# The seam between an expert stage and an attention: queries and scores earlier, transposes later, last down products in two parts

## The chip, the cores and the metric

The kernel runs on one core of one Trainium2 chip. The core has TensorE (PE in the rows; PEld is its weight load), VectorE (DVE), ScalarE (ACT), GpSimd (POOL) and SyncE (SP), which issues most transfers. The engines run side by side and wait for one another by semaphores. The metric is the time of one launch in microseconds on the device; three runs of the kernel before gave 2293.72, 2294.40 and 2299.11 us, median 2294.4.

## The reference

The program is four residual layers on x, four batches of 512 tokens with 512 channels, in float32. The change lies between the second and the third.

```python
x = x + xattn0(layernorm(x), ctx)                      # layer 1: channel attention
xf = layernorm(x)                                      # layer 2: mixture of experts
top_p, top_i = top_k(softmax(xf @ gate_w.T), 2)        #   8 experts, 2 per token, inner width 352
y = sum_e combine[:, e] * (silu(xf @ fc1[e].T) * (xf @ fc2[e].T)) @ proj[e].T
x = x + y + sigmoid(xf @ shared_gate_w.T) * shared(xf)
q = layernorm(x) @ Wq                                  # layer 3: cross-attention, 16 heads of 128
k, v = ctx @ Wk, ctx @ Wv                              #   8 key heads, each for 2 query heads
x = x + softmax(mask(q @ k.T / sqrt(128))) @ v @ Wo
x = x + ffn(layernorm(x))                              # layer 4
```

## The kernel before, in words

**Precision.** Every product is made of three matmuls (`product`, L81 to L86): each operand is split into a high and a low part, high = a rounded copy, low = operand minus high. So each operand costs one copy (mostly ScalarE) and one subtraction (VectorE or GpSimd), and TensorE waits for the second.

**The expert stage** (`sparse_experts`) walks over 24 tiles of sorted tokens: two of 256 slots (two sub-tiles), then one of 128, and so on; tile 23, the last, is small. In step t TensorE does gate and up products of tile t, turns the gathered rows of tile t + 1, and does the down products of tile t - 1, sub-tile by sub-tile. A small tile's hidden values come out the other way round and are transposed (`turn_hidden`, L1686) before ScalarE's `hidden_high` and VectorE's `hidden_low` split them. Each down result is copied by ScalarE (`copy_y`) and stored. A `nc.Block()` ends with a barrier of all engines.

**The third layer's first part** (`cross_attention`, to the loop over head groups) has on TensorE 48 units of six matmuls (`key_value`), which make the keys and values that were not made earlier: per batch 4 value units (half 0), 4 key units, 4 value units (half 1). ScalarE copies each result from its PSUM bank to one of five stages (`kv_copy`) and SyncE stores it to DRAM. Units use four banks in turn, and from unit 40 two.

Beside them runs the layer norm of 16 token tiles. GpSimd gathers the two expert results of a tile (`gather_y`, a ring of four tiles), VectorE adds them to x and takes the statistics (`add_experts`, `stats`), GpSimd makes root and shift for four tiles at once (`rstd`), ScalarE normalises (`norm`), TensorE transposes (`turn_x`, L172: turn t), ScalarE and VectorE split (`high`, `low`). `turned_after(n)` says which turn follows unit n: before, turn 0 follows unit 15 and one comes every second unit, so turn 15 follows unit 45. VectorE does `low(i - 8)` behind the addition of tile i (`LAG` = 8), and turn t (t >= 4) waits for `low(t - 4)`. `BEFORE_Q` = 44 is the unit ahead of which the 24 matmuls of the first two queries stand.

Behind the units come three scores, their masked maxima (`masked_max`), exponentials and normalisations, and then the group loop: eight units of attention per group (`body`), each with four scores, four turns of probabilities (L2398), one weighted-value product and half of a query. The V of each pair of heads is loaded back from DRAM, `load_kv`; pair 1 is loaded when all stages have been stored.

## Time and profile before

| quantity | value |
|---|---|
| runs of the kernel before | 2293.72, 2294.40, 2299.11 us |
| the profiled execution: its own time | 2292.79 us |
| its span, first to last instruction | 2291.0 us |
| TensorE busy | 2227.5 us (97%), 11073 matmuls |
| VectorE busy | 1430.7 us (62%) |
| ScalarE busy | 1050.4 us (46%) |
| GpSimd busy | 471.5 us (21%) |
| mean granted TensorE clock | 0.996 |

The page shows one profiled execution. In the timelines a row gives start, duration, engine, line and operation, what it writes and reads, and in brackets how long its engine had been idle and who ended that. Matmuls overlap: each lasts some 0.39 us in the rows, but the next starts 0.23 us after it at full clock. The same tile name may stand for several uses: `route_kv_hi` is the high half of the context, later of a K/V pair; `route_weights` holds weights, stages, normalised rows and probabilities.

### The profile page before, as it was taken

The page shows a single profiled execution, that of the slowest core. Times are in us where ns is not written, and L with a number is a line of the kernel's source. Part 1 is how long each engine was busy: PE and PEld are TensorE (multiplying, and loading weights), DVE is VectorE, ACT ScalarE, POOL GpSimd, SP SyncE. Part 2 cuts the span into 40 slices and gives each one's busy share as a digit, 9 for nine tenths or more (in the row PEclk, how much of TensorE's full clock was granted, in tenths as well). Part 3 has the DMA queues.
Part 4 walks back from the last instruction along what each step waited for, and adds up shares of the span by engine and source line. Part 5 has one row for each costly group of instructions (what it writes and reads, how often), then busy time and mean ns, then how long its engine had stood idle before and what let it go on. Part 6 is the DMA issues. An engine that isn't in the chain of part 4 may idle for free. (4 is left out here: it accounts for less than half of the span.)

```text
span 2291.0 us, 32147 instructions
## 1 busy us (share of the span) xinstructions
PE 2227.5 (97%) x11073; PEld 1851.7 (81%) x11073; DVE 1430.7 (62%) x2979; ACT 1050.4 (46%) x1872; POOL 471.5 (21%) x448
## 2 busy tenths in 40 slices
PE   7999999998999989999999999999998999999999
PEld 5777788887999967888888888888877888888887
DVE  6854365545777775777767777677776555565544
ACT  5532210104565556666666666666664322323221
POOL 4434455401111172100010000100031202121000
PEclk9999999999999999999999999999999999999999
DMA  6422321115777775101101000101002233232331
GB/s 223 137 97 53 102 57 33 28 58 187 285 277 264 267 261 200 46 19 38 37 19 45 27 27 27 30 25 37 28 10 75 80 108 102 97 123 75 111 115 51
DMA packets 92539, 222.33 MB, mean 97 GB/s; under 512 B 9616, under 2 KB 30608, under 8 KB 89360
## 3 DMA queue, kind: packets, MB, share of 16 engines
q1 hardware_dynamic: 84112, 193.65, 24.7%
q0 software_dynamic: 8320, 27.27, 4.7%
q8 instruction: 65, 1.06, 0.2%
q14 instruction: 42, 0.34, 0.0%
HBM read 176.85 MB, written 44.04 MB: 96 GB/s over the span
## 5 line engine op out<-in xcount | busy, mean ns | idle before, releaser
L2055 ACT ACTIVATE route_weights<-route_weights,xa_minus_max 128x512 f32<-128x512 f32 x256 | 184.9, 722 | 193.4 <-DVE xa_minus_max L2203 193.3
L2219 DVE TENSOR_TENSOR xa_late_hi<-xa_ps_t,route_wv_hi 128x512 fp32r<-128x512 f32 x256 | 175.0, 683 | 128.6 <-ACT route_wv_hi L2064 128.5
L1990 POOL TENSOR_TENSOR route_kv_lo<-route_rows,route_kv_hi 128x1024 fp32r<-128x1024 f32 x32 | 76.9, 2402 | 717.4 <-ACT route_kv_hi L2029 717.3
L2064 ACT ACTIVATE route_wv_hi<-xa_ps_t 128x512 fp32r<-128x512 f32 x256 | 151.2, 591 | 105.7 <-PE xa_ps_t L2398 71.1
L2203 DVE CUSTOM_DVE_ANT_0 route_weights<-xa_ps_s,route_mask_bias 128x512 f32<-128x512 f32 x256 | 175.8, 687 | 1.1 <-issue 0.4
L2398 PEld LDWEIGHTS xa_ps_t<-ident,route_weights 128*128 128x128 f32 x1024 | 126.2, 140 | 44.1 <-issue 9.1
L2398 PE MATMUL xa_ps_t<-ident,route_weights 128*128 128x128 f32 x1024 | 153.9, 273 | 5.5 <-DVE xa_late_hi L2219 4.8
L2765 ACT ACTIVATE ffn_silu<-ffn_ps_gate,late_scales 128x512 f32<-128x512 f32 x64 | 44.0, 688 | 248.9 <-PE ffn_ps_gate L86 248.9
L84 PE MATMUL xa_ps_p<-route_wv_hi,route_kv_hi 128*128 128x512 f32 x284 | 119.2, 420 | 4.5 <-DVE xa_late_lo L2241 2.9
L2581 DVE TENSOR_TENSOR route_kv_lo<-route_weights,route_kv_hi 128x1024 fp32r<-128x1024 f32 x42 | 53.7, 1279 | 101.7 <-ACT route_kv_hi L2576 101.6
L1044 ACT ACTIVATE moe_silu<-moe_ps_gate 128x512 f32<-128x512 f32 x44 | 26.3, 597 | 197.4 <-PE moe_ps_gate L86 197.4
L84 PE MATMUL ex_ps_h<-ex_xT_hi,ex_w_hi 128*128 128x256 f32 (+1 forms) x384 | 110.0, 287 | 6.5 <-DVE ex_xT_lo L1626 6.5
L84 PE MATMUL xa_ps_p<-late_xT_hi,late_wq_hi 128*128 128x512 f32 x256 | 111.8, 437 | 2.8 <-DVE late_wq_lo L2188 2.8
L86 PE MATMUL xa_ps_p<-route_wv_hi,route_kv_lo 128*128 128x512 f32 x284 | 112.1, 395 | 0.0
L85 PE MATMUL ex_ps_h<-ex_xT_lo,ex_w_hi 128*128 128x256 f32 (+1 forms) x384 | 109.5, 285 | 0.0
L86 PE MATMUL ex_ps_h<-ex_xT_hi,ex_w_lo 128*128 128x256 f32 (+1 forms) x384 | 108.9, 284 | 0.0
L84 PE MATMUL xa_ps_s<-route_kv_hi,xa_q_hi 128*128 128x512 f32 x256 | 104.6, 409 | 2.9 <-DVE xa_minus_max L2203 2.1
L84 PE MATMUL xa_ps_o<-xa_late_lo 128*128 128x512 f32 x256 | 103.4, 404 | 3.8 <-DVE late_xT_lo L2631 2.4
L2225 DVE TENSOR_TENSOR x<-xa_ps_o,x 128x512 f32<-128x512 f32 x128 | 87.6, 684 | 28.4 <-PE xa_ps_o L86 28.4
L1428 POOL DMA_INDIRECT route_rows<-moe_xn,route_slot_token x40 | 44.7, 1118 | 282.1 <-PE ex_ps_t L1679 234.4
L85 PE MATMUL xa_ps_p<-xa_late_hi,route_kv_hi 128*128 128x512 f32 x256 | 101.9, 398 | 0.0
L86 PE MATMUL xa_ps_s<-route_kv_hi,xa_q_lo 128*128 128x512 f32 x256 | 101.5, 396 | 0.0
(507 smaller groups left out, 6642.4 us busy)
## 6 DMA issues: line engine op xcount, KB each, us to landing
route_weights<-in_ffn_w SPq DMA_DIRECT2D x64, 512.0 KB, 3.7
route_weights<-in_expert_w SPq DMA_DIRECT2D x12, 1408.0 KB, 6.5
ex_w_raw<-in_expert_w SPq DMA_DIRECT2D x12, 1408.0 KB, 6.4
route_weights<-wd_folded SPq DMA_DIRECT2D x64, 256.0 KB, 2.6
moe_y<-ex_y SPq DMA_DIRECT2D x40, 256.0 KB, 3.4
route_weights<-in_expert_w SPq DMA_DIRECT2D x12, 768.0 KB, 8.9
ex_w_raw<-in_expert_w SPq DMA_DIRECT2D x12, 768.0 KB, 8.1
route_weights<-in_xa_w SPq DMA_DIRECT2D x18, 512.0 KB, 3.6
```

The lines of the kernel that those rows point to most:

```text
L84: pe.matmul(out, lh, rh, start=start, stop=False)
L85: pe.matmul(out, lh, rl, start=False, stop=False)
L86: return pe.matmul(out, ll, rh, start=False, stop=stop)
L1428: pool.indirect_dma_start(out=G.rows[:, at:at + C], out_offset=None, in_=G.xn_dram, in_offset=bass.IndirectOffsetOnAxis(ap=G.slot_token[:, ...
L1990: pool.tensor_tensor(kvl[b % 2][:], rawkv[b % 2], f32(kvh[b % 2][:]), ALU.subtract).then_inc(M.kv_ready, 1)
L2055: act.activation(prob[slot][:], prob[slot][:], ACT.Exp, bias=nmx[:, slot:slot + 1], scale=-1.0, accum_out=tot[:, slot:slot + 1]).then_inc( ...
L2064: act.activation(PTh[:, :, tt * P:(tt + 1) * P], psT[tt % 2][:].rearrange("p (k n) -> p k n", k=TT), ACT.Copy).then_inc(M.pt_hi, 1)
L2203: dve.tensor_tensor_reduce(out=prob[slot][:], in0=psS[slot % 2][:], in1=maskb[:, b * S:(b + 1) * S], scale=-SCALE, scalar=3.4e38, op0=ALU. ...
L2219: dve.tensor_tensor(PTl[:, :, tt * P:(tt + 1) * P], psT[tt % 2][:].rearrange("p (k n) -> p k n", k=TT), f32(PTh[:, :, tt * P:(tt + 1) * P] ...
L2225: dve.tensor_tensor(x[:, t, :], psO[tt % 2][:], x[:, t, :], ALU.add).then_inc(M.x_added, 1)
L2398: last = pe.transpose(psT[tt % 2][:, k * P:(k + 1) * P], prob[tt][:, k * P:(k + 1) * P], ident)
L2581: dve.tensor_tensor(L.gu_lo[s % 3][:], final_raw(G, s)[0], f32(L.gu_hi[s % 3][:]), ALU.subtract).then_inc(L.gu_ready, 1)
```

## The change

The parts, as the code has them:

- Last expert tile: the down products of tile 22 are split around the transpose of tile 23's hidden values, whose two halves lie in a buffer of their own. ScalarE splits the value weights in two halves, the first ahead of the copy of sub-tile 1; VectorE makes the first half's remainder (`first_lo`) before the block ends. The two mask operations move into tiles 21 and 22.
- Unit 0 no longer waits for a weight remainder made in the new block.
- The gather ring has five tiles instead of four; root b is made ahead of the gather of tile 4b + 7 instead of behind it; the context's low halves of batches 2 and 3 are made by VectorE instead of GpSimd.
- Stages 3 and 4 and the normalised rows lie in `late_rows`, so the four probability buffers are free during the units.
- Turn 0 follows unit 20, turn 15 unit 46, evenly spread. The norms of tiles 12 to 15 are done by VectorE.
- The queries stand ahead of unit 38, the first two scores and their softmax behind unit 40, the third behind unit 42. Two banks serve from unit 34: up to 39 the score banks, from 40 the query banks.
- ScalarE starts its block with an exponential of one column.

The count of matmuls is the same. First the last down products on TensorE (`ex_ps_hT` is the transposed hidden tile, `ex_ps_y` a down result), before:

```order
L84 MATMUL ex_ps_y<-ex_w_hi,ex_hidden_hi 128x512
L85 MATMUL ex_ps_y<-ex_w_lo,ex_hidden_hi 128x512
L86 MATMUL ex_ps_y<-ex_w_hi,ex_hidden_lo 128x512
L1686 MATMUL ex_ps_hT<-ident,ex_hidden 128x128 x3
L84 MATMUL ex_ps_y<-ex_w_hi,ex_hidden_hi 128x512
```

and now:

```order
L84 MATMUL ex_ps_y<-ex_w_hi,ex_hidden_hi 128x512
L85 MATMUL ex_ps_y<-ex_w_lo,ex_hidden_hi 128x512
L86 MATMUL ex_ps_y<-ex_w_hi,ex_hidden_lo 128x512
L84 MATMUL ex_ps_y<-ex_w_hi,ex_xT_hi 128x512
L85 MATMUL ex_ps_y<-ex_w_lo,ex_xT_hi 128x512
```

The transpose stood between the last matmuls of sub-tile 1 and the last tile's product; it has gone from there to the front of the nine matmuls of sub-tile 1, and the last product reads its own buffer.

Second, VectorE at the end of the units (`late_xT_lo` is a turned tile's low part, `xa_q_lo` a query's), before:

```order
L161 TENSOR_TENSOR late_xT_lo<-xa_ps_t,late_xT_hi 128x4x128 x2
L2197 TENSOR_TENSOR xa_q_lo<-xa_ps_p,xa_q_hi 128x512 x2
L161 TENSOR_TENSOR late_xT_lo<-xa_ps_o,late_xT_hi 128x4x128 x2
L2202 MEMSET xa_idle 128x1
L2203 ISA route_weights,xa_minus_max<-xa_ps_s,route_mask_bias 128x512
```

and now:

```order
L2241 TENSOR_TENSOR xa_q_lo<-xa_ps_p,xa_q_hi 128x512 x2
L155 TENSOR_SCALAR late_rows<-x,xa_ln_mean_var,xa_ln_rstd 128x512
L161 TENSOR_TENSOR late_xT_lo<-xa_ps_o,late_xT_hi 128x4x128
L155 TENSOR_SCALAR late_rows<-x,xa_ln_mean_var,xa_ln_rstd 128x512
L161 TENSOR_TENSOR late_xT_lo<-xa_ps_t,late_xT_hi 128x4x128
L2246 MEMSET xa_idle 128x1
L2247 ISA route_weights,xa_minus_max<-xa_ps_s,route_mask_bias 128x512
```

The first maximum stood behind the low parts of all 16 tiles; now it stands behind that of tile 12, and VectorE's norms stand between.

Third, GpSimd's gathers and roots (L125 is the first of a root's four instructions, L130 its last), before:

```order
L1996 DMA late_rows<-moe_y,route_slot 128x512 x4
L1774 TENSOR_TENSOR route_kv_lo<-route_rows,route_kv_hi 128x1024
L125 TENSOR_SCALAR xa_ln_var_eps<-xa_ln_mean_var 128x4
L126 TENSOR_TENSOR xa_ln_rstd<-xa_ln_var_eps,xa_ln_minus_half 128x4
```

and now:

```order
L2040 DMA xa_q_hi<-moe_y,route_slot 128x512
L2040 DMA xa_q_lo<-moe_y,route_slot 128x512
L125 TENSOR_SCALAR xa_ln_var_eps<-xa_ln_mean_var 128x4
L126 TENSOR_TENSOR xa_ln_rstd<-xa_ln_var_eps,xa_ln_minus_half 128x4
L129 TENSOR_TENSOR xa_ln_shift<-xa_ln_mean_var,xa_ln_rstd 128x4
L130 TENSOR_SCALAR xa_ln_shift<-xa_ln_shift 128x4
L2040 DMA xa_q_hi<-moe_y,route_slot 128x512
```

The context's low half has left this queue, and one gather (two transfers) now stands behind the root.

The diff, cut to its core:

```diff
...
+        late_hidden = xh[1 - LAST.p][:].rearrange("p k n -> p (k n)")
+        last_hh, last_hl = (late_hidden[:, i * FCH * P:(i + 1) * FCH * P].rearrange("p (f n) -> p f n", f=FCH)
...
+        def small_hidden(t):
+            return (last_hh, last_hl) if isinstance(t.n, int) and t.n == LAST.n else (hh[:, :, 0:P], hl[:, :, 0:P])
...
-                def copy_y(t):
-                    for u in range(t.subs):
+                def copy_y(t, subs=None):
...
                 def hidden_high(t):
                     act.wait_ge(M.hT_done, t.smalls + 1)
-                    act.wait_ge(M.y_done, t.subs_before)
-                    act.activation(hh[:, :, 0:P], psX[:, 0:FCH * P].rearrange("p (f n) -> p f n", f=FCH),
...
                         copy_y(t.after(-1))
+                    if which == "last":
+                        copy_y(t.after(-1), [0])
                     if t.small:
                         hidden_high(t)
                     if which == "last":
-                        half = KV * GROUPS * D
                         act.wait_ge(G.wv_loaded, 16 * KV)
-                        act.activation(G.wvh[:], G.weights[:, half:2 * half], ACT.Copy).then_inc(G.wkv_hi, 1)
+                        act.activation(value_half(G.wvh[:], 0), value_half(raw_values(G), 0), ACT.Copy).then_inc(G.wkv_hi, 1)
+                        copy_y(t.after(-1), [1])
+                        act.activation(value_half(G.wvh[:], 1), value_half(raw_values(G), 1), ACT.Copy).then_inc(G.wkv_hi, 1)
...
+                    if t.j == LAST.j - 2:
+                        dve.wait_ge(M.mask_loaded, 16)
+                        dve.reduce_max(G.any_key[:], mask8[:].rearrange("p (b s) -> p b s", b=B), axis=AX.X)
+                    if t.j == LAST.j - 1:
+                        dve.tensor_scalar(G.mask_bias[:], mask8[:], MASKED, -MASKED, ALU.mult, ALU.add)
...
-                dve.wait_ge(M.mask_loaded, 16)
-                dve.tensor_scalar(G.mask_bias[:], mask8[:], MASKED, -MASKED, ALU.mult, ALU.add)
-                dve.reduce_max(G.any_key[:], mask8[:].rearrange("p (b s) -> p b s", b=B), axis=AX.X)
+                dve.wait_ge(G.wkv_hi, 1)
+                dve.tensor_tensor(first_values(G), value_half(raw_values(G), 0), f32(value_half(G.wvh[:], 0)), ALU.subtract)
...
-                def down(t):
+                def down(t, subs=None):
                     pe.wait_ge(M.hidden_ready, t.steps_before + t.steps)
                     pe.wait_ge(M.down_ready, t.n + 1)
                     pe.wait_ge(M.y_copied, t.subs_before + SUBS)
...
-                    if which != "first":
+                    if which == "middle":
                         down(t.after(-1))
+                    if which == "last":
+                        down(t.after(-1), [0])
                     if t.small:
                         turn_hidden(t)
+                    if which == "last":
+                        down(t.after(-1), [1])
...
         prob = [G.weights[:, NQ + i * S:NQ + (i + 1) * S] for i in range(4)]
-        STAGES = 5
...
+        STAGES = len(stage)
...
+        wkl = late_lo[:, 0:NK]
+        wvl = [first_values(G), late_lo[:, NW:NW + 2 * S].rearrange("p (k n) -> p k n", k=KV)]
...
         KVS = B * PER
-        BEFORE_Q = KVS - 4
-        FIRST_TURN = KVS - 2 * NT - 1
+        BEFORE_Q = KVS - 10
+        AFTER_Q = BEFORE_Q + 2
...
         def kv_bank(n):
+            if n >= AFTER_Q:
+                return psP[n % 2]
             return psS[n % 2] if n >= BEFORE_Q - 4 else (psP + psS)[n % 4]
...
-            return (n - FIRST_TURN) // 2 if n >= FIRST_TURN and (n - FIRST_TURN) % 2 == 0 and n < KVS - 1 else None
+            spread = [FIRST_TURN + t * (KVS - 2 - FIRST_TURN) // (NT - 1) for t in range(NT)]
+            return spread.index(n) if n in spread else None
+        def turn_before(n):
+            return max(turned_after(m) for m in range(n) if turned_after(m) is not None)
...
                 for u in range(SUBS):
...
-                for t in range(RING):
+                for t in range(NT):
+                    if t >= TT and t % TT == TT - 1:
+                        rstd(t // TT - 1)
                     gather_y(t)
-                for b in range(B):
-                    for t in range(RING + b * TT, min(RING + (b + 1) * TT, NT)):
-                        gather_y(t)
-                    if 2 <= b + 1 < B:
-                        context_low(pool, G, b + 1)
-                    rstd(b)
+                rstd(B - 1)
                 kv_low(0, 0)
...
+                act.activation(idle[:, 0:1], ident[:, 0:1], ACT.Exp)
...
                     if t is not None:
                         high(t)
-                        if t + 2 < NT:
+                        if t + 2 < BY_VECTOR:
                             norm(t + 2)
                     if n == PER + 4:
                         split_q(0, 0)
                         split_q(0, 1)
-                    if n == BEFORE_Q:
+                    if n == BEFORE_Q - 2:
                         kv_high(1, 0)
+                    if n == BEFORE_Q - 1:
+                        act.wait_ge(M.y_taken, NT)
                         proj_high(FIRST_Q, qh[0])
-                    if n == BEFORE_Q + 1:
                         proj_high(SECOND_Q, qh[1])
-                for t in range(3):
-                    exp(t, t)
-                normalise(0, 1)
+                    if n == AFTER_Q:
+                        exp(0, 0)
+                        exp(1, 1)
+                        normalise(0, 1)
+                    if n == AFTER_Q + 2:
+                        exp(2, 2)
...
-                dve.wait_ge(G.wkv_hi, 1)
-                for half in range(2):
-                    lo, raw, hi = (v.rearrange("p (k two n) -> p k two n", k=KV, two=2)[:, :, half, :]
-                                   for v in (wvl, rw[:, NW:HEAD], wvh))
-                    dve.tensor_tensor(lo, raw, f32(hi), ALU.subtract).then_inc(M.wkv_ready, 1)
                 dve.wait_ge(G.wkv_hi, 2)
+                dve.tensor_tensor(wvl[1], value_half(raw_values(G), 1), f32(value_half(wvh, 1)),
+                                  ALU.subtract).then_inc(M.wkv_ready, 1)
+                dve.wait_ge(G.wkv_hi, 3)
                 dve.tensor_tensor(wkl, rw[:, 0:NK], f32(wkh), ALU.subtract).then_inc(M.wkv_ready, 1)
...
+                def first_softmax():
+                    masked_max(0, 0, 0)
+                    masked_max(1, 1, 0)
+                    normalise(0, 0, 0)
+                    invert(1, 1).then_inc(M.inv_ready, 1)
                 for i in range(NT + LAG):
                     if i < NT:
...
                         split_q(0, 0)
                         split_q(0, 1)
                     if i >= LAG:
                         low(i - LAG)
-                    if i == NT + LAG - 3:
+                    if i >= LAG and turn_before(BEFORE_Q) == i - LAG:
                         proj_low(FIRST_Q, qh[0], ql[0])
                         proj_low(SECOND_Q, qh[1], ql[1])
-                for n in range(KVS - STAGES, KVS):
-                    stored(dve, n)
-                dve.wait_ge(R.xn_turned, NT)
-                for t in range(3):
-                    masked_max(t, t, 0)
-                normalise(0, 0, 0)
-                invert(1, 1).then_inc(M.inv_ready, 1)
+                    if i >= LAG and turn_before(AFTER_Q + 1) == i - LAG:
+                        first_softmax()
+                    if i >= LAG and turn_before(AFTER_Q + 3) == i - LAG:
+                        masked_max(2, 2, 0)
+                    if i >= LAG and BY_VECTOR <= i - LAG + 3 < NT:
+                        dve.wait_ge(R.xn_ready, i - LAG + 3)
+                        norm(i - LAG + 3)
                 def body(g, which):
...
-                    if n in (0, TT):
-                        pe.wait_ge(M.wkv_ready, 3 if n else 1)
-                    if n >= BEFORE_Q - 4:
+                    if n == TT:
+                        pe.wait_ge(M.wkv_ready, 2)
+                    if AFTER_Q <= n < AFTER_Q + 2:
+                        pe.wait_ge(M.proj_ready, SECOND_Q.n + 1)
+                    elif n >= BEFORE_Q - 4:
                         pe.wait_ge(M.kv_out, n - 1)
...
-                pe.wait_ge(M.kv_out, KVS)
-                pe.wait_ge(M.proj_ready, SECOND_Q.n + 1)
-                pe.wait_ge(M.kv_ready, 1)
-                for t in range(3):
-                    scores(t, t, 0, 0)
-                pe.wait_ge(R.xT_ready, NT)
+                    if n == AFTER_Q:
+                        pe.wait_ge(M.kv_out, AFTER_Q)
+                        pe.wait_ge(M.kv_ready, 1)
+                        scores(0, 0, 0, 0)
+                        scores(1, 1, 0, 0)
+                    if n == AFTER_Q + 2:
+                        scores(2, 2, 0, 0)
+                pe.wait_ge(R.xT_ready, NT - 2)
...
+                            if which == "first" and ul == 0:
+                                pe.wait_ge(M.kv_out, KVS)
+                                pe.wait_ge(R.xT_ready, NT)
...
```

## Rows read from the trace of the kernel before

**Rows 1.** timeline of TensorE; start us, us, line, operation; in brackets its wait

```profile
808.18 0.50 PE L84 MATMUL ex_ps_y<-ex_w_hi,ex_hidden_hi 128*128 128x512 f32 x1 [1.33 <-DVE ex_hidden_lo L1631]
...
813.44 0.71 PE L84 MATMUL xa_ps_p<-route_wv_hi,route_kv_hi 128*128 128x512 f32 x1 [2.91 <-DVE xa_late_lo L2241]
...
840.24 0.66 PE L172 MATMUL xa_ps_t<-ident,route_weights 128*128 128x128 f32 x4 [2.71 <-ACT route_weights L2078]
...
855.74 0.63 PE L172 MATMUL xa_ps_t<-ident,route_weights 128*128 128x128 f32 x4 [0.84 <-ACT route_weights L2078]
...
871.32 0.91 PE L172 MATMUL xa_ps_t<-ident,route_weights 128*128 128x128 f32 x4 [2.27 <-ACT route_weights L2078]
...
905.08 0.50 PE L84 MATMUL xa_ps_s<-route_kv_hi,xa_q_hi 128*128 128x512 f32 x1 [0.78 <-ACT route_weights L2039]
...
908.24 0.50 PE L84 MATMUL xa_ps_s<-route_kv_hi,xa_q_hi 128*128 128x512 f32 x1 [1.49 <-DVE xa_minus_max L2203]
...
910.60 0.66 PE L2398 MATMUL xa_ps_t<-ident,route_weights 128*128 128x128 f32 x4 [0.69 <-DVE route_weights L2214]
...
913.47 0.63 PE L2398 MATMUL xa_ps_t<-ident,route_weights 128*128 128x128 f32 x4 [0.37 <-DVE xa_late_hi L2219]
```

**Rows 2.** stretches: us, busy us of each engine, PEclk, DMA, GB/s

```profile
813.40:816.90 3.50, 3.46 (x8) 2.79 (x9) 2.17 (x2) 0.58 (x1) 2.29 (x3) 0.51 0.94 334
...
1732.50:1736.00 3.50, 3.42 (x19) 2.99 (x20) 2.42 (x5) 2.50 (x4) 0.00 (x0) 1.00 0.00 0
```

**Rows 3.** timeline of TensorE: turns, queries, last unit, fourth scores, first weighted product

```profile
859.18 0.60 PE L172 MATMUL xa_ps_t<-ident,route_weights 128*128 128x128 f32 x4
...
862.41 0.60 PE L172 MATMUL xa_ps_o<-ident,route_weights 128*128 128x128 f32 x4
...
892.60 0.48 PE L84 MATMUL xa_ps_p<-late_xT_hi,late_wq_hi 128*128 128x512 f32 x1
...
898.15 0.39 PE L84 MATMUL xa_ps_s<-route_wv_hi,route_kv_hi 128*128 128x512 f32 x1
...
909.04 0.40 PE L84 MATMUL xa_ps_s<-route_kv_hi,xa_q_hi 128*128 128x512 f32 x1
...
918.90 0.49 PE L84 MATMUL xa_ps_p<-route_wv_hi,route_kv_hi 128*128 128x512 f32 x1
```

**Rows 4.** timeline of ScalarE and VectorE around the block boundary

```profile
806.56 0.60 ACT L1565 ACTIVATE ex_y<-ex_ps_y 128x512 f32<-128x512 f32 x1 [1.47 <-PE ex_ps_y L86]
...
809.18 2.28 DVE L1670 TENSOR_REDUCE route_any_key<-ex_mask 128x4 f32<-128x2048 uint8 x1
...
810.57 0.60 ACT L1565 ACTIVATE ex_y<-ex_ps_y 128x512 f32<-128x512 f32 x1 [1.22 <-PE ex_ps_y L86]
...
811.95 1.06 ACT L2068 ACTIVATE xa_late_hi<-route_weights 128x1024 fp32r<-128x1024 f32 x1 [0.78 <-PEq L1504]
```

**Rows 5.** timeline of GpSimd and VectorE, and one group of GpSimd's lines

```profile
835.86 0.26 POOL L125 TENSOR_SCALAR xa_ln_var_eps<-xa_ln_mean_var 128x4 f32<-128x4 f32 x1
...
845.35 0.75 DVE L2232 SCALAR_TENSOR_TENSOR x<-xa_q_hi,route_weight,x 128x512 f32<-128x512 f32 x1 [2.42 <-DMA xa_q_lo<-moe_y,route_slot]
...
865.12 2.91 DVE L2232 SCALAR_TENSOR_TENSOR x<-xa_q_hi,route_weight,x 128x512 f32<-128x512 f32 x1
...
L1996 POOL DMA_INDIRECT late_rows<-moe_y,route_slot x16 | 16.0, 1002 | 4.9 <-issue 4.3 <-DVEq L2234 0.6
```

**Rows 6.** costliest groups of the page: maximum and exponential

```profile
L2203 DVE CUSTOM_DVE_ANT_0 route_weights<-xa_ps_s,route_mask_bias 128x512 f32<-128x512 f32 x256 | 175.8, 687 | 1.1 <-issue 0.4
...
L2055 ACT ACTIVATE route_weights<-route_weights,xa_minus_max 128x512 f32<-128x512 f32 x256 | 184.9, 722 | 193.4 <-DVE xa_minus_max L2203 193.3
```

**Rows 7.** ScalarE's last copy, V load issued 907.0 to 907.9, second K/V split

```profile
904.35 0.69 ACT L2039 ACTIVATE route_weights<-xa_ps_s,route_any_key 128x512 f32<-128x512 f32 x1 [0.35 <-PE xa_ps_s L86]
...
route_rows<-xa_v SPq DMA_DIRECT2D x1, 256.0 KB, 3.2
...
915.31 1.05 ACT L2029 ACTIVATE route_kv_hi<-route_rows 128x1024 fp32r<-128x1024 f32 x1
```

62 lines of the change are left out of this document (38 added, 24 removed).

## The prediction

> **What bounds the kernel now.** The idle times of TensorE come first. Over the span of 2291.0 us it is busy 97%, and between 808 and 914 us, where the expert tiles give way to the second attention, it stands still nine times for 13.4 us in all (1.33+2.91+2.71+0.84+2.27+0.78+1.49+0.69+0.37) [rows 1]. The reader is to see what ends each: the last hidden part, the value-weight remainder behind the block boundary, three normalised tiles (turns 0, 4, 8), the last copy, and the softmax of the first scores. Second, the table by stretches: in the 3.50 us behind the gap of 2.91 us the granted clock is 0.51, PE's 1.2 GHz level, which loses 3.50 x (1 - 0.51) = 1.7 us; yet behind 1732.5, where PE had also stood still (the stretch begins in that gap), it is 1.00 [rows 2]. Third, the undisturbed pace: 24 query matmuls take 898.15 - 892.60 = 5.55 us, so a unit of six takes 1.39; two units and a turn take 862.41 - 859.18 = 3.23, so a turn costs 0.45 [rows 3]. The matmuls behind 840.24 and 871.32 (gaps of 2.71 and 2.27 us) are slow too; I price them like the first, 5.1 us in all. So 18.5 us can be won here at most. Everything behind is one PE-bound stream, so what is won by its first weighted-value product (918.90, 9.9 us behind the fourth scores at 909.04) reaches the end [rows 3].
>
> **The down products in two parts.** The last hidden transpose is turned one sub-tile earlier; the 9 matmuls of sub-tile 1 (9 x 0.23 = 2.1 us) hide its split. But the last product also waits until sub-tile 1 has been copied. That copy started at 806.56 [rows 4]; now the 3 transposes stand ahead of those 9 matmuls, so it starts near 806.95, ends at 807.55, and the last product starts at 807.65 instead of 808.18. The 1.33 us wait becomes 0.85: gain 0.5. The following copy (810.57), the store behind it and the barrier move by the same 0.5, and engines start again at 811.45 instead of 811.95 [rows 4]. VectorE's two mask operations (the reduction 2.28 us, the bias about half of it [rows 4]) go into tiles 21 and 22 of the expert stage. VectorE waited there for the down products (PE works ahead by more than a tile), so I cost them at nothing; without that cover it would be 3.5 us.
>
> **The block boundary.** Unit 0 now needs only what was split before the barrier. PE can start at 811.45, not 813.44. Its gap is about 1.5 us, like the 1.49 of 908.24, behind which nothing slowed [rows 1]. Gain 2.0, of which 0.5 is the above, and 1.7 of clock.
>
> **Transposes from unit 20, roots one gather sooner.** Without waits unit 20 ends at 811.45 + 21 x 1.39 = 840.7. Root 0 is issued after gather 6 (14 gathers of 1.0 + 0.3 us from 813.5, i.e. 832.4) and takes 3.5 us (from 835.86 to the norm ahead of turn 0 at 840.24, 0.8 us long): 836 [rows 1, 5]. ScalarE's norm follows unit 19's copy and is done at 840.9. So turn 0 costs 0.2 instead of 2.7 + 1.7. Turn 4: root 1 is ready at about 849, PE comes at 851.0: nothing. Turn 8 is the weak place. It comes after unit 33, at 811.45 + 34 x 1.39 + 8 x 0.45 = 862.4. It waits for root 2 (stats of tile 11) and for VectorE's low part of tile 4, which VectorE issues behind the addition of tile 12. Its rate: tile 8 at 845.35, tile 13 at 865.12, i.e. 19.8 us for five tiles, in which lie 2.2 us of a stretched addition, 1.3 of weight splitting and 0.6 of a data wait, so 3.3 us per tile [rows 5]. In the new order tile 7's gather stands behind root 0, so tile 8 starts at 845.2 all the same; then 4 more tiles x 3.3 + 1.3 (weights) + 1.3 (context split, now on VectorE) puts low 4 at 864.3. Turn 8 waits 1.9 us. Turns 9 and 10 find low 5 and 6 just ready (867.6, 870.9). Bounds of this term: 0, if tile 8 comes 2 us sooner, and 2.3 plus a clock fall of 1.7, the present one [rows 1, 2].
>
> On VectorE and GpSimd together: the addition at 865.12 lasted 2.91 us beside GpSimd's context split, against 0.75 alone [rows 5]. Both such stretches (2 x 2.2 us) go, since the context splits move to VectorE (2 x 1.3). One new overlap appears: GpSimd's split of the first keys (2.4 us) starts right behind root 3, just when VectorE's norm of tile 12 is released by that root. The Trainium skill (SBUF — State Buffer, Who interferes with whom) says that the two engines share a port pair as an exclusive lock, and that tensor_scalar can take it in its two-port mode; the stretched addition agrees, a norm on VectorE is not in this trace. By that rule norm 12 would wait 2.3 us and unit 40 about 0.5. I bound it from the rows at 0 to 2.2 and take 0.5 by the stretched addition, since 1.7 us of slack stand before unit 40.
>
> **Queries and scores ten units from the end.** Turn 10 ends at 871.4, the queries at 876.9, units 38 and 39 with turn 11 at 880.2, unit 40 at 881.6 + 0.5 = 882.1. Behind it PE has seven units, four turns and three scores of 0.70: 9.8 + 1.8 + 2.1 = 13.7 us. ScalarE works in order, and its copy of unit 41 stands behind two exponentials and a normalisation, each waiting on VectorE: maximum 0.69, exponential 0.72 [rows 6]. Turn 12, its two splits, maximum, exponential, inverse, normalise chain to about 5.3 us behind unit 40; with two banks unit 43 then waits 0.2. The third exponential, behind norm 15 and low 13, is done at +9.3; copy 43 follows and unit 45 waits 0.8. So 1.0 us, and the fourth scores start at 882.1 + 14.7 = 896.8 instead of 909.04. Bounds: 0 (PE was not stopped in the present last eight units) and 3 (one more softmax latency of 1.5 as at 908.24, twice).
>
> **What is late next.** Now the last copy and the attention are adjacent. K and V of pair 1 can be loaded only when the last values are stored. Last copy at 904.35, V load issued at about 907.6, landed 3.2 us later, so 6.5 us behind the copy; ScalarE used it at 915.31, 6.3 us behind the fourth scores [rows 7]. Without the softmax jam ScalarE gets there 5.8 us behind them, but the data come only 0.2 + 6.5 = 6.7 behind. ScalarE waits 0.9 us, and everything behind it in its queue (two transposed copies, an exponential) with it; PE waits for the last of these before the first weighted product: 10.2 us behind the fourth scores instead of 9.9. So that product starts at 907.0 instead of 918.90: a gain of 11.9 us. Bounds of this wait: 0 and 2.5.
>
> **The sum** is made against the profiled execution: 918.90 - 907.0 = 11.9 us, off its 2292.8 us (1.8 more than its span). That execution is 1.6 below the median shown, 2294.4; so 2294.4 - 11.9 = **2282.5**. The account by waits agrees: 18.5 in, and 0.85 + 1.5 + 0.2 + 1.9 + 0.5 + 1.0 + 0.3 = 6.3 out, 12.2 net. ScalarE's table load also moves, from the first exponential to the block start, where ScalarE would otherwise wait for its first copy; it costs nothing in either place.
>
> **Rivals.** (a) The waits that I add do not come: VectorE is 2 us earlier, the V load hides. Gain 11.9 + 1.9 + 0.5 + 1.0 + 0.3 = 15.6: 2279. For it: only estimates of 1 to 2 us stand behind these; against it: VectorE's rate is set by work, not by waits. (b) The clock falls in two of the new gaps (1.5, 1.9 us), 3.2 us, and turn 8 waits 1 longer: gain 7.7, 2286.7. For it: all three gaps from 2.27 to 2.91 us fell; against: 1.49 did not, nor did the one at 1732.5 [rows 1, 2]. (c) VectorE or the roots set the pace of turns 8 to 11, by 1.0 us more than 3.3 per tile over eight tiles, 8 us: gain 4, 2290.5. The gathers' landing, which VectorE already waits for, would show it; so would the mask work stopping PE in the expert stage (3.5). (d) Slower. From unit 34, not 40, only two banks are left, and ScalarE in its one queue carries copies, turned halves, the key split and exponentials. If every one of these 14 units waits for the copy two before it, PE loses 14 times the lateness of ScalarE; at 0.85 us per unit the gain is gone, at 1.4 (19.6 us) it is slower by over 0.3%: 2302. Against it: in the present last eight units with two banks and a turn on every second PE never waited for a copy before 905.08 [rows 1].
>
> **Chances.** Forecast 0.47 (own range 2280 to 2286), (a) 0.17, (b) 0.18, (c) 0.12, (d) 0.06. About 0.3%, 6.9 us, is what a measurement of this kernel can tell from no change: faster is below 2287.5. Faster: 0.47 + 0.17 + 0.6 of (b) + 0.2 of (c) = 0.77; same 0.17; slower 0.06. The range for 8 in 10: from 2277, which takes in (a), to 2290, through (b) to the middle of (c).
>
> **What would show it.** Right: PE starts 1.5 us behind its last expert product at full clock; turn 0 with under 0.5 us of wait; one wait of 1 to 3 us at turn 8, ended by the low part of tile 4 or the norm; fourth scores near 897; ScalarE waiting for a DMA before the second K/V split. Wrong: a granted clock of 0.5 anywhere between 811 and 910; waits for copies on many units from 34; TensorE idle between 785 and 802; or a first weighted product before 904 or after 912.

## The result, and the profile after

| kernel | runs | median us | lowest to highest |
|---|---|---|---|
| before | 8 | 2294.06 | 2289.43 to 2299.11 |
| changed | 8 | 2285.94 | 2280.16 to 2289.88 |

The ratio is 0.9963, 95% interval 0.9951 to 0.9975: 8.5 us faster (5.7 to 11.2). Two more series of the same kernel gave 0.9953 [0.9940, 0.9966] and 0.9959 [0.9945, 0.9974]. The forecast was 2282.5 us, a gain of 11.9; its direction and range held.

The profiled execution of the changed kernel is the slowest of its eight (2289.88 us, span 2288.1). I measure from the start of the last expert product (the matmul of 811.06 below) to the first weighted-value product (913.15), as the forecast did; I call it the stretch. Before the change it took 918.90 - 808.18 = 110.7 us [rows 1, 3]. TensorE's waits in the stretch of the changed kernel (start, duration, operation, in brackets the wait), and the fourth scores:

```profile
811.06 0.47 PE L84 MATMUL ex_ps_y<-ex_w_hi,ex_xT_hi 128*128 128x512 f32 x1 [0.78 <-ACT ex_y L1574]
...
814.82 0.47 PE L84 MATMUL xa_ps_p<-route_wv_hi,route_kv_hi 128*128 128x512 f32 x1 [1.44 <-PEq L1513]
...
837.43 0.79 PE L84 MATMUL xa_ps_p<-route_wv_hi,route_kv_hi 128*128 128x512 f32 x1 [4.39 <-ACT late_rows L2080]
...
898.22 0.50 PE L84 MATMUL xa_ps_p<-route_wv_hi,route_kv_hi 128*128 128x512 f32 x1 [0.15 <-ACT late_rows L2080]
...
902.93 0.39 PE L84 MATMUL xa_ps_s<-route_kv_hi,xa_q_hi 128*128 128x512 f32 x1
...
906.73 0.63 PE L2450 MATMUL xa_ps_t<-ident,route_weights 128*128 128x128 f32 x4 [0.68 <-DVE xa_late_hi L2263]
...
913.15 0.50 PE L84 MATMUL xa_ps_p<-route_wv_hi,route_kv_hi 128*128 128x512 f32 x1 [0.56 <-DVE xa_late_hi L2263]
```

The stretch is 913.15 - 811.06 = 102.1 us. The first two waits are the forecast's (0.85 and 1.5). None stands at turns 0, 4 and 8. But one of 4.39 us, the largest, was in no part of the forecast. The table by stretches (us, busy us of PE, PEld, DVE, ACT, POOL with counts, granted clock, DMA share, GB/s) shows the clock behind it, and in three places outside:

```profile
31.80:35.20 3.40, 3.40 (x14) 2.79 (x13) 2.87 (x7) 0.43 (x1) 1.27 (x2) 0.51 0.39 138
151.30:154.70 3.40, 3.40 (x12) 2.68 (x11) 3.12 (x6) 3.08 (x6) 0.00 (x0) 0.51 0.00 0
...
837.40:840.80 3.40, 3.37 (x8) 2.69 (x9) 2.94 (x7) 3.06 (x5) 2.76 (x5) 0.50 0.75 259
1687.20:1690.60 3.40, 3.36 (x10) 2.83 (x11) 3.06 (x11) 3.30 (x6) 2.61 (x3) 0.52 0.00 0
```

Each such fall to half (TensorE's 1.2 GHz level) costs by this estimate 3.40 x 0.5 = 1.7 us. In the trace of before the same three outer places stand at 1.00. So the two executions compare as 2.9 us (2291.0 - 2288.1) = 8.6 of the stretch, less 2.9 ahead of it (two falls, 3.4), less 2.8 after it (one fall, 1.7).

The fall does not account for all that is lost after the stretch. From the first weighted-value product to the end of the span it is 2291.0 - 918.90 = 1372.1 us before. In the six traces of changed kernels (those of the experiments below) without a fall there it is 1373.4 to 1373.5, in the seven with one 1374.7 to 1375.0. So a fall costs 1.2 to 1.6 us there, and each of the 13, start_only too, gives back some 1.3 us besides. The last matmul, before and then in the second trace of the changed kernel, which has no fall there and its first weighted-value product at 907.85:

```profile
2287.40 0.39 PE L86 MATMUL ffn_ps_y<-ffn_down_hi,ffn_hidden_lo 128*128 128x512 f32 x1
```

```profile
2277.69 0.39 PE L86 MATMUL ffn_ps_y<-ffn_down_hi,ffn_hidden_lo 128*128 128x512 f32 x1
```

2287.40 - 918.90 = 1368.50, and 2277.69 - 907.85 = 1369.84. Matmul by matmul the loss grows little by little through the attention (0.56 us after 407 us, 1.34 after 910) and then stays. Its cause is open, and there is one trace of before only.

What held ScalarE, whose copy TensorE waited for (timelines of ScalarE, then of SyncE's queue):

```profile
817.13 1.39 ACT L2080 ACTIVATE route_weights<-xa_ps_p,route_any_key 128x512 f32<-128x512 f32 x2
...
825.52 0.60 ACT L2080 ACTIVATE route_weights<-xa_ps_p 128x512 f32<-128x512 f32 x1 [2.96 <-DMA xa_v<-route_weights]
...
836.69 0.69 ACT L2080 ACTIVATE late_rows<-xa_ps_p,route_any_key 128x512 f32<-128x512 f32 x1 [5.92 <-remote]
```

```profile
818.51 0.33 SPq L1787 DMA_DIRECT2D route_weights<-in_xa_w  x1
818.88 0.43 SPq L1978 DMA_DIRECT2D late_h<-in_h  x1
819.36 0.44 SPq L1979 DMA_DIRECT2D late_tables<-in_ffn_tables  x1
819.85 1.50 SPq L2001 DMA_DIRECT2D xa_v<-route_weights  x3
```

The copy of unit 0 was done at 817.8, but its store was issued at 819.85, behind the query loads, which wait for VectorE's splits. Unit 5 needs unit 0's stage again, and waits 2.96 us. Unit 9 then waits 5.92 us; the trace names no transfer ("remote").

### The profile page after: what moved, and what is told of

It reads as the page before. It is cut to its first block and busy times, and to the rows that moved or that the text cites. A ratio compares the mean times of both kernels' runs of the same rounds, so it can differ in the third digit from the quotient of the medians.

```text
span 2288.1 us, 32149 instructions
## 1 busy us (share of the span) xinstructions
PE 2230.0 (97%) x11073; PEld 1852.4 (81%) x11073; DVE 1432.6 (63%) x2985; ACT 1048.8 (46%) x1870; POOL 466.0 (20%) x446
## 2 busy tenths in 40 slices
DMA packets 92539, 222.33 MB, mean 97 GB/s; under 512 B 9616, under 2 KB 30608, under 8 KB 89360
## 5 line engine op out<-in xcount | busy, mean ns | idle before, releaser
L2638 DVE TENSOR_TENSOR route_kv_lo<-route_weights,route_kv_hi 128x1024 fp32r<-128x1024 f32 x42 | 53.7, 1279 | 101.8 <-ACT route_kv_hi L2633 101.6
L84 PE MATMUL xa_ps_o<-route_first_lo,xa_late_lo 128*128 128x512 f32 x256 | 103.8, 406 | 3.8 <-DVE late_xT_lo L2688 2.4
L86 PE MATMUL xa_ps_p<-late_xT_hi,late_wq_lo 128*128 128x512 f32 x256 | 102.0, 398 | 0.0
L86 PE MATMUL xa_ps_o<-route_first_lo,xa_late_lo 128*128 128x512 f32 x256 | 101.2, 395 | 0.0
```

What stands on the lines that cost most here:

```text
L84: pe.matmul(out, lh, rh, start=start, stop=False)
L86: return pe.matmul(out, ll, rh, start=False, stop=stop)
L2638: dve.tensor_tensor(L.gu_lo[s % 3][:], final_raw(G, s)[0], f32(L.gu_hi[s % 3][:]), ALU.subtract).then_inc(L.gu_ready, 1)
```

## The experiments

Four kernels of one set ran on one chip beside the kernel before. "Stretch" is as above; "turn 8" is its start behind the last expert product; "hold" the sum of TensorE's waits between 20 and 30 us behind that product, turns left out, with f where a clock fall follows.

| kernel | ratio, 95% interval | stretch | turn 8 | hold |
|---|---|---|---|---|
| before | 1 | 110.7 | 63.1 | 0 |
| changed, first trace | 0.9963 [0.9951, 0.9975] | 102.1 | 60.9 | 4.4 f |
| set 1: again (changed) | 0.9953 [0.9940, 0.9966] | 99.9 | 58.1 | 1.1 |
| late_loads | 0.9959 [0.9946, 0.9971] | 97.2 | 55.9 | 0 |
| eight_stages | 0.9959 [0.9946, 0.9972] | 98.4 | 57.0 | 0 |
| unit0_waits | 0.9972 [0.9962, 0.9982] | 101.6 | 60.3 | 0 |
| set 2: turns_before | 0.9961 [0.9947, 0.9974] | 100.7 | 57.1 | 1.7 |
| queries_late | 0.9956 [0.9940, 0.9972] | 98.9 | 58.5 | 2.9 |
| whole_down | one run | 102.6 | 61.5 | 4.5 f |
| best | 0.9959 [0.9945, 0.9974] | 103.1 | 63.5 | 4.7 f |
| set 3: third (changed) | 0.9959 [0.9945, 0.9974] | 99.4 | 58.2 | 2.9 |
| relieved | 0.9967 [0.9954, 0.9980] | 100.3 | 59.1 | 2.3 f |
| turns_queries | 0.9974 [0.9962, 0.9985] | 101.6 | 57.4 | 3.0 f |
| start_only | 0.9998 [0.9987, 1.0008] | 108.4 | 63.0 | 4.0 |

An interval is some 3 us to each side, so only the ratio of the last kernel stands apart. Those of turns_queries and unit0_waits are the highest of the rest, but their intervals overlap the changed kernel's. The traces must tell the rest, and each is one execution. In best turn 0 and so turn 8 stand later by the edit itself.

**The changed kernel again.** No edit.

> The changed kernel once more. In its first trace ScalarE waited 5.9 us before 836.7 for a stage of the keys and values to be stored, TensorE then stood still 4.39 us and lost about 1.6 more to the lower clock. Theory A (the stores of the first units leave late and run behind, so five stages are too few; it happens in every execution): this trace has such a wait again, 2 to 6 us in all between units 5 and 12, and the time is near 2286. Theory B (one transfer was late in that one execution): no such wait here, though the time is near 2286 all the same.

Measured: 2283.08 us against 2293.86. The trace has such waits again. ScalarE waited for stores eleven times between units 5 and 19, for 12.9 us in all; the first and the last:

```profile
822.41 0.60 ACT L2080 ACTIVATE route_weights<-xa_ps_p 128x512 f32<-128x512 f32 x1 [2.93 <-DMA xa_v<-route_weights]
...
843.08 0.60 ACT L2080 ACTIVATE late_rows<-xa_ps_s 128x512 f32<-128x512 f32 x1 [1.89 <-DMA xa_v<-late_rows]
```

TensorE, which runs up to four banks ahead, saw little of it, and then waited at turn 0, whose normalised tile stood behind those copies in ScalarE's queue:

```profile
835.18 0.50 PE L84 MATMUL xa_ps_p<-route_kv_hi,xa_late_hi 128*128 128x512 f32 x1 [1.10 <-ACT route_weights L2080]
...
844.43 0.66 PE L172 MATMUL xa_ps_t<-ident,late_rows 128*128 128x128 f32 x4 [1.64 <-ACT late_rows L2118]
```

So theory B (one late transfer in one execution) is out, and theory A is right in kind; the 4.39 us of the first trace are not the usual size.

**Late loads.**

```diff
-                sp.wait_ge(M.wkv_ready, 2)
-                load_q(sp, io, G, 0)        # and the two constants
                 for n in range(KVS):
                     sp.dma_start(to, stage[n % STAGES][:]).then_inc(kv_stored[n % STAGES], 16)
+                    if n == 8:
+                        sp.wait_ge(M.wkv_ready, 2)
+                        load_q(sp, io, G, 0)    # and the two constants
```

> The changed kernel with the loads of the query weights and of two constants issued behind the store of unit 8 instead of ahead of the store of unit 0. In the changed kernel the first stage was copied at 817.8 and its store issued only at 819.85, since these loads wait for a split of VectorE and stand ahead in SyncE's queue. Theory A: the stores start 2 us sooner and have 0.6 MB less beside them; the wait for a stage goes, and with it 4.4 us and the clock fall of 1.6: 4 to 6 us below the changed kernel, about 2280 to 2282. Theory B: no difference in the time. Theory C (the gathers, which take half of what the DMA engines move, are what delays the stores): the wait becomes shorter by 1 to 2 us at most.

**Eight stages.**

```diff
-        stage = [...] + L.row[0:2]
-        STAGES = len(stage)
+        stage = [...] + L.row[0:2] + prob[0:3]
+        STAGES = 5
+        DEEP = len(stage)
+        DEEP_END = 3 * DEEP
...
+        def slot(n):
+            return n % DEEP if n < DEEP_END else (n - DEEP_END) % STAGES
...
-                    sp.dma_start(to, stage[n % STAGES][:]).then_inc(kv_stored[n % STAGES], 16)
+                    sp.dma_start(to, stage[slot(n)][:]).then_inc(kv_stored[slot(n)], 16)
```

> The changed kernel with eight stages instead of five for the first 24 units (three probability buffers serve as stages until then), the order of all work unchanged. Theory A: the copy of unit 9 waits for the store of unit 1 and not of unit 4, some 4.2 us more of slack; the wait of TensorE goes or stays below 0.5 us: 4 to 6 us below the changed kernel. Theory B: no difference. Theory C: as A at first, but the backlog of stores grows for as long as the gathers run, and a wait of 1 to 3 us comes later, between units 12 and 24.

Measured: both remove the hold and shorten the stretch, by 2.7 and 1.5 us against the kernel again; the time of neither can be told from it (2282.64 and 2284.89 us against 2283.08), so the 4 to 6 us of theory A did not come. Nor did the later wait for stores of theory C. In late_loads the V stores out of `route_weights` land 5.6 us behind their issue in the median, not 6.6. Where the saving of eight_stages goes, its next wait shows (the first row is of late_loads, the second of eight_stages):

```profile
841.98 0.66 PE L172 MATMUL xa_ps_t<-ident,late_rows 128*128 128x128 f32 x4 [1.15 <-ACT late_rows L2119]
```

```profile
866.97 0.66 PE L172 MATMUL xa_ps_t<-ident,late_rows 128*128 128x128 f32 x4 [2.13 <-DVE late_xT_lo L161]
```

The first is turn 0. The second is turn 8, waiting for the low part of tile 4: TensorE comes earlier and meets VectorE.

**Unit 0 waits.**

```diff
-                    if n == TT:
+                    if n in (0, TT):
                         pe.wait_ge(M.wkv_ready, 2)
```

> The changed kernel with unit 0 waiting once more for the splits that VectorE makes behind the block boundary, as it did before the change. This takes away the early start alone. By my forecast's account the start is worth 1.5 us of wait and 1.7 of clock: about 3.2 to 5 us slower than the changed kernel (the splits end near 818.5, so PE starts some 3.5 us later). Theory A says that the early start is given back by the wait for a stage: that wait shrinks by what the start is later, so the time is within 2 us of the changed kernel's.

```profile
814.20 0.77 PE L84 MATMUL xa_ps_p<-route_wv_hi,route_kv_hi 128*128 128x512 f32 x1 [5.25 <-DVE xa_late_lo L2285]
```

```profile
811.20:818.00 6.80, 3.81 (x9) 3.06 (x10) 1.74 (x2) 2.27 (x4) 4.35 (x5) 0.51 0.90 305
```

The edit takes away more than the early start: unit 0 now waits for the remainders of the second value half and of the keys, where before it waited for that of the first value half. The start comes 814.20 - 806.62 = 7.6 us behind the last expert product, 3.8 later than in the changed kernel and 2.3 later than before the change. Of the 6.8 us at half clock TensorE works 3.81 (second row), which loses 1.9: 5.7 in all. In this trace the stretch grows by 1.7 only, and no store is waited for between units 5 and 19 (the V stores out of `route_weights` land after 5.0 us in the median). The 4.0 us in between are mostly waits that a late TensorE doesn't have: 1.10, 1.64 and one of 0.58 behind the scores in the trace again, 3.3 together. So in this execution most of the early start is given back, as theory A has it. The times lean the other way: 2286.55 us against 2283.08 for the kernel again, 3.5 more, which is within the forecast's 3.2 to 5. The profiled execution (2283.45) is among the fastest of twelve, which reach to 2292.44. What the start is worth beside the other parts therefore stays open.

**Turns as before; queries late; both.**

```diff
-        FIRST_TURN = PER + 8
-            spread = [FIRST_TURN + t * (KVS - 2 - FIRST_TURN) // (NT - 1) for t in range(NT)]
+        FIRST_TURN = PER + 3
+            spread = [FIRST_TURN + 2 * t for t in range(NT)]
```

```diff
-        BEFORE_Q = KVS - 10
+        BEFORE_Q = KVS - 5
```

> The changed kernel with the turns where they were before: turn 0 behind unit 15, one every second unit. This takes away the later turns alone (the root stays one gather sooner, the queries stay ahead of unit 38). My forecast gave the turns 2.7 + 1.7 at turn 0 and 2.3 + 1.7 at turn 8. With the start and the root as they are now, TensorE is at turn 0 some 26.0 us behind its last expert product (3.8 us of boundary and 16 units of 1.39), the normalised tile about 28.0 behind it: I expect a wait of 2 us at turn 0, one of 2 to 3 at turn 8, with one or two clock falls of 1.7, together 5 to 7 us slower than the changed kernel. The rival (VectorE's rate alone sets when turns 8 to 11 are through, wherever turn 0 stands) says that the waits move but their sum does not: within 2 us of the changed kernel.

> The changed kernel with the queries five units from the end instead of ten, the first two scores behind unit 45 and the third behind unit 47, all else unchanged. This takes away the early softmax. My forecast: the softmax latency stands open again between the last unit and the group loop, as the waits of 1.49, 0.69 and 0.37 us in the kernel before [rows 1], and the last copies come late; 2 to 3.5 us slower than the changed kernel, without a clock fall. The rival (the forecast's fourth: two banks and ScalarE's queue make the early place dear) says that it costs nothing or even gains up to 1 us.

> The changed kernel with both the turns (behind unit 15, every second unit) and the queries (five units from the end, third score behind the last unit) moved back, the early start, the sooner roots, the ring of five, the split down products and the work moved to VectorE kept. Undone singly, turns and queries cost nothing that could be measured (0.9961 and 0.9956 of the kernel before, against 0.9953 to 0.9963 for the changed kernel). If each covers for the other, both together cost 3 to 6 us; if neither matters once the start and the roots are early, the stretch stays at 99 to 101 us and the time within 2 us of the changed kernel.

Of turns_before the waits at turns 0 and 8:

```profile
840.73 0.66 PE L172 MATMUL xa_ps_t<-ident,late_rows 128*128 128x128 f32 x4 [1.73 <-ACT late_rows L2118]
...
867.58 0.66 PE L172 MATMUL xa_ps_t<-ident,late_rows 128*128 128x128 f32 x4 [0.48 <-DVE late_xT_lo L161]
```

Neither has a clock fall behind it, and each edit alone stays inside the intervals (0.9961, 0.9956). So the 5 to 7 us forecast for the turns are out and their rival holds. For the queries 2 to 3.5 us were forecast, about the width of the interval; nothing in the ratio or the stretch (98.9) shows a loss, so there too the rival fits better. Both together give 0.9974, against 0.9953 to 0.9963: 2 to 5 us, but its interval overlaps theirs. That each covers for the other is thus suggested by the ratios and not shown: of the 2.2 us between the stretches of turns_queries and third (101.6, 99.4) the clock fall behind the hold alone makes about 1.5.

**The down products in one piece** (whole_down). Both sub-tiles are multiplied and copied ahead of the last hidden tile, as before.

```diff
-                    if which == "middle":
+                    if which != "first":
                         down(t.after(-1))
-                    if which == "last":
-                        down(t.after(-1), [0])
...
-                        down(t.after(-1), [1])
```

> The changed kernel with the down products of tile 22 in one piece again: both sub-tiles' products ahead of the transposes of tile 23, both copies ahead of its high part. By my forecast TensorE waits for the last hidden part 1.33 us again (0.78 in the changed kernel), and the last product starts 0.5 us later against the product before it. The rival says that the buffer of its own for the last hidden values gives that half microsecond, not the split of the products: the wait stays below 1.0.

```profile
807.07 0.50 PE L84 MATMUL ex_ps_y<-ex_w_hi,ex_xT_hi 128*128 128x512 f32 x1 [1.33 <-DVE ex_xT_hi L1642]
```

1.33 against 0.78 in all traces with the split: the split gives the half microsecond, not the buffer.

**An attempt at a better one.** Eight stages, late loads, and turn 0 behind unit 22 (`FIRST_TURN = PER + 10`).

> The changed kernel with eight stages for the first 24 units, the query loads behind the store of unit 8, and turn 0 behind unit 22 instead of 20 (turn 15 stays behind unit 46). With the stores out of the way what is left between 811 and 910 us are the waits of turn 0 (1.15 us with late loads) and of turn 8 (2.13 with eight stages). Turn 0 comes 2.8 us later and turn 8 comes 1 unit later (1.4 us): waits of 0 and 0.7. Theory A with this: the stretch from the last expert product to the first weighted-value product, 99.9 us in the second trace of the changed kernel, shortens to 96 to 96.5, and the time is 2 to 4 us below the changed kernel's: 2279 to 2281. The rival: VectorE's rate decides, the late turns crowd at the end, and as much is waited there: no difference.

```profile
835.09 0.69 ACT L2087 ACTIVATE route_weights<-xa_ps_p,route_any_key 128x512 f32<-128x512 f32 x1 [7.22 <-remote]
```

It is not better: 0.9959. In its trace ScalarE stood 7.22 us ahead of unit 9, although unit 9 needs only the store of unit 1. That had been issued before 818.4. Up to 826 SyncE's queue had been given the last expert store (0.26 MB), two contexts of 0.52 and eight stores of 0.26, together 3.41. The DMA views of 812 to 828 and of 812 to 835 say that it had moved all but one store's worth of this by 828, and by 835 all that had been given since as well (4.28):

```profile
q1 hardware_dynamic: 1439, 3.15, 52.4%
```

```profile
q1 hardware_dynamic: 2136, 4.28, 50.1%
```

(queue, packets, MB, share.) If the queue moves in about the order of issue, the store of unit 1 was written long before 835, so the bytes ahead of it don't explain this hold, and theory A doesn't either. Whether one of the 16 DMA engines lagged behind the others the views don't tell.

**Relieved.** Eight stages, late loads, a ring of four, and the context of batch 3 behind the store of unit 12:

```diff
-                for b in range(2, B):
-                    sp.wait_ge(G.ctx_ready, b - 1)
-                    load_context(sp, io, G, b, b % 2)
+                sp.wait_ge(G.ctx_ready, 1)
+                load_context(sp, io, G, 2, 0)
...
+                    if n == PER:
+                        sp.wait_ge(G.ctx_ready, 2)
+                        load_context(sp, io, G, 3, 1)
```

> The changed kernel a third time, as the measure for the other three on the same chip. The stretch from the last expert product to the first weighted-value product took 102.1 us in its first trace and 99.9 in its second. In five of the ten traces so far (the first of the changed kernel, and four kernels that ran on another chip) ScalarE was held for 3 to 7 us about unit 9 and landings are missing from the trace; four of these five stood in a row on one chip. If that is a state of the chip or of the execution, this trace has either both marks or neither; if it comes from the kernel alone, all four kernels of this set that load the DMA engines as this one does have it.

> The changed kernel with fewer transfers in the first 15 us of the block: eight stages for 24 units, the query loads behind the store of unit 8, the context of batch 3 behind the store of unit 12, and a gather ring of four tiles. Theory F (the DMA engines are full, 412 to 416 GB/s, and then a store takes 10 us and more to land, whatever the number of stages: in the kernel with eight stages, late loads and late turns ScalarE waited 7.2 us for a store issued 15 us before): with 0.5 MB less in that stretch no such wait, stretch 97 to 99 us, and 1 to 4 us below the changed kernel on the same chip. The rival (that hold is a disturbance from outside and comes with any kernel): the wait can come here too, and the times are equal.

```profile
830.62 0.50 PE L84 MATMUL xa_ps_p<-route_wv_hi,route_kv_hi 128*128 128x512 f32 x1 [2.28 <-ACT route_weights L2090]
```

The hold is there with less to move, the stretch is 100.3 us instead of 97 to 99, and the time (2287.15 us) is not below the changed kernel's, so theory F falls. The changed kernel's third series gave 2285.83 us against 2293.41; its trace has the hold (1.67 + 1.19 us at 23.6 and 26.5 us behind the last expert product) and no times at which stores landed. The same goes for all four traces of this set. For one and the same code the trace again has landing times and a hold of 1.10 us; the first and the third have none, and holds of 4.39 and 2.86. So it is not a thing of the kernel alone.

**The start alone.** The kernel turns_queries (turns and queries both moved back) with, besides, the roots behind the gather again, a ring of four, and the context's low halves on GpSimd. The diff against turns_queries, cut to GpSimd's part:

```diff
                 for t in range(NT):
-                    if t >= TT and t % TT == TT - 1:
-                        rstd(t // TT - 1)
                     gather_y(t)
+                    if t >= TT and t % TT == TT - 1:
+                        if t // TT >= 2:
+                            context_low(pool, G, t // TT)
+                        rstd(t // TT - 1)
```

> The last kernel with the roots behind the gather again, a ring of four tiles, and the context's low halves on GpSimd: of the change only the split down products, the early start, the new buffers and the norms of tiles 12 to 15 on VectorE are left. My forecast gives the start and the down products 4.2 us (0.5 + 2.0 + 1.7), so about 2289.5 by it, with waits of 2.5 to 4.7 us at turn 0 (PE comes 2 us earlier, the root at the same time) and 2 at turn 8, each with a clock fall. The rival that VectorE and the roots set the end whatever the start says that the early start is waited away at turn 0, and the gain is below 2 us.

```profile
840.38 0.66 PE L172 MATMUL xa_ps_t<-ident,late_rows 128*128 128x128 f32 x4 [1.73 <-ACT late_rows L2121]
...
855.09 0.63 PE L172 MATMUL xa_ps_t<-ident,late_rows 128*128 128x128 f32 x4 [1.59 <-ACT late_rows L2121]
...
870.65 1.09 PE L172 MATMUL xa_ps_t<-ident,late_rows 128*128 128x128 f32 x4 [2.31 <-ACT late_rows L2121]
```

```profile
869.42 0.24 POOL L130 TENSOR_SCALAR xa_ln_shift<-xa_ln_shift 128x4 f32<-128x4 f32 x1
```

The ratio is 0.9998: nothing is left of the gain. The waits of before are back at turns 0, 4 and 8 [rows 1], and turn 8 starts 870.65 - 807.62 = 63.0 us behind the last expert product, before 63.1. It waits for root 2, whose last row (the second fence) starts 61.8 us behind it, before 61.9; in the trace again that root's last row is

```profile
861.45 0.24 POOL L130 TENSOR_SCALAR xa_ln_shift<-xa_ln_shift 128x4 f32<-128x4 f32 x1
```

53.5 us behind it, 8.3 sooner. So the parts, one on top of the other: the start alone 0 (0.9998), with GpSimd's new order, ring and context split 5.5 us (0.9974), with the turns and queries 3.7 more (0.9958, the mean of the three series). The first step is clear of the intervals (that of start_only begins at 0.9987, that of turns_queries ends at 0.9985); the second is not. Which of the three edits on GpSimd's side brings the roots forward was not tried by itself.

## Why the prediction was right, step by step

Times are counted from the last expert product, forecast at 807.65.

- **Down products:** 0.85 us of wait forecast, 0.78 measured, 1.33 without the split. Right.
- **Boundary:** start 3.80 behind, gap 1.5, full clock; measured 3.76, 1.44, and no slow matmul. The operation is right, its price, 2.0 (in which the 0.5 of the down products is) + 1.7 = 3.7, is no gain of its own: start_only has it and gains nothing. (The 4.2 in the expectation of start_only counts the 0.5 twice.) It pays only because the roots come sooner as well. The sum could use it, since it counted along the path of all parts together; as an account part by part it misleads.
- **Turn 8:** low 4 at 864.3, that is 56.7 behind, and a wait of 1.9. In eight_stages, where nothing else is late, turn 8 starts at 57.0 with 2.13 of wait, ended by that low part, and turns_before and turns_queries meet it at 57.1 and 57.4. So VectorE's chain was sized well, with some luck. The printed sum, 845.2 + 4 x 3.3 + 1.3 + 1.3, is 861.0; 864.3 takes a fifth tile, since low 4 stands behind the addition of tile 12. And with the 0.6 of data wait left out the rate is 3.1 us per tile, not 3.3. In late_loads turn 8 starts at 55.9 without a wait, so the chain itself moves by 1 us. In the changed kernel TensorE comes at 58.1 to 60.9 and doesn't wait.
- **Turn 0:** 0.2 forecast; 0 or 1.64, and then because ScalarE was held, not for the root. (Root 0's issue is 831.7 by the forecast's own 14 x 1.3, not 832.4; nothing hangs on it.)
- **VectorE and GpSimd together:** the key split and the norm of tile 12 met as forecast. The norm lasts 0.55 us alone:

```profile
878.98 2.40 POOL L2034 TENSOR_TENSOR route_kv_lo<-route_rows,route_kv_hi 128x1024 fp32r<-128x1024 f32 x1 [0.20 <-ACT route_kv_hi L2070]
...
879.18 2.48 DVE L155 TENSOR_SCALAR late_rows<-x,xa_ln_mean_var,xa_ln_rstd 128x512 f32<-128x512 f32 x1 [0.70 <-PE xa_ps_o L172]
...
887.78 0.55 DVE L155 TENSOR_SCALAR late_rows<-x,xa_ln_mean_var,xa_ln_rstd 128x512 f32<-128x512 f32 x1 [1.91 <-PE xa_ps_o L172]
```

  So it was stretched by 1.9 us, within the bounds of 0 to 2.2. TensorE lost none of it, 0.5 forecast: the slack hid it all. The Trainium skill (SBUF — State Buffer, Who interferes with whom) calls this an exclusive lock of a shared port pair, by which the forecast named 2.3; these rows agree, the norm ends 0.3 us behind GpSimd's split.
- **ScalarE's order in units 41 to 45:** 1.0 forecast, 0.15 measured (at 898.22). The first scores were made at 889.3, 78.2 behind, and no copy was late by more; the fourth rival (two banks) is wrong.
- **Fourth scores:** 89.15 behind; measured 89.1 in the second and third trace, 91.9 in the first.
- **The V load:** 0.9 us of wait on ScalarE, the weighted product 10.2 us behind the fourth scores; measured

```profile
909.54 1.06 ACT L2070 ACTIVATE route_kv_hi<-route_rows 128x1024 fp32r<-128x1024 f32 x1 [0.88 <-DMA route_rows<-xa_v]
```

  and 913.15 - 902.93 = 10.2 (10.8 in the second trace, 10.2 in the third). Right.
- **The stretch:** 99.35 forecast; 102.1, 99.9 and 99.4 measured.
- **After the stretch:** the forecast lets all that is won reach the end. 1.3 us of it do not: the stretch is 10.8 and 11.4 us shorter in the second and third trace, less 1.3 that is 9.5 and 10.1, and the three ratios say 9.6 on the mean. Nothing in the forecast stands for this term.

Of the forecast's own signs of being wrong one came: a granted clock of 0.5 between 811 and 910, in the first trace (837.4), and not in the second and third. The first weighted product at 913.15, past the 912 named, starts late mostly because the execution was 3.4 us late already at the last expert product. Copies were not waited for on many units from 34, and TensorE did not stand still ahead of that product, so the mask work was free as forecast.

What the sum lacks besides is the way of the stages out to memory. I read ScalarE's wait for them in the trace of before as zero and took it to stay so, though a stage comes round again every five units, 7 us, against 4.8 to land. The start moved the units 2 us ahead of SyncE's queue, and its loads and its wait for VectorE stayed where they were. With the hold this cost 1.1 to 4.4 us (in the second trace also 1.64 at turn 0) and in one trace of three a fall of 1.7. How much of it is the stores and how much the hold is not told apart. Terms that did not come (turn 8's 1.9, 0.5, and 0.85 of ScalarE's 1.0) stand against it, so the stretch came out right in two traces partly by offset, which is luck. The chance of "faster" was well placed; the time, 3.4 us too low, is within the interval of two of the three series.

What stays open: where the rest of the hold comes from, how often it is there, and where the 1.3 us after the stretch go. Also open is how the medians relate to single traces: three of the stretch's clock falls in the one trace of before made 5.1 of the 11.9 us.

## What to carry to other kernels

When a stage starts earlier, list every ring behind it (copy, store, reuse) and compare its period with the landing time; the queue that serves it must start earlier too. Price parts on one path together, and then ask of each what it gives alone: the first engine to be released gains nothing while the next meeting point stays where it was. Find these meeting points (here turn 8, at 56 to 57 us with the sooner roots and at 63 without) and forecast them; they are steadier than the waits, which move about in front of them. And compare the rest of the program too, from a common matmul to the end: a change can cost a little where nothing was meant to move.

## What was not expected of the hardware

- **A hold without a visible cause.** In nine of the fourteen traces the view of transfers has no landing times for the stores in this stretch, and in all nine TensorE stood 1.7 to 4.7 us between 20 and 30 us behind the last expert product. In the five that have them it stood 0 to 1.1 us. For the same code, first trace and the trace again:

```profile
xa_v<-route_weights SPq DMA_DIRECT2D x7, 256.0 KB
```

```profile
xa_v<-route_weights SPq DMA_DIRECT2D x7, 256.0 KB, 6.6
```

  The transfers' own packets are recorded alike in all fourteen (92539 or 92540, 222.33 MB), so it is the landings alone that are missing. Whether their records are lost because the chip is held, or recording holds it, no run here tells. It came with all four kernels of two sets and with none of the first.
- **Clock falls.** Of eleven waits of 2.27 us and more in the stretch ten were followed by a fall, that of 2.60 us in start_only (at 837.00) by none; of the waits up to 2.13 us none was. This is a count over these traces, not a rule. With the waits of 5.25 and 4.65 us came falls of twice the length, 6.8 us, which begin inside the wait; the second:

```profile
834.10:840.90 6.80, 5.07 (x12) 4.06 (x13) 5.64 (x10) 4.06 (x6) 5.33 (x7) 0.51 0.82 270
```
